# A transformer tower on one core: fewer constant products at the start, first loads on two queues, and one product for centring and gate

## The chip, the core and the metric

The kernel runs on one core of a Trainium2 chip. A core has TensorE (matrix products into PSUM), VectorE, ScalarE, GpSimd and SyncE (SP), each with its own instruction queue, and 16 DMA engines that they share. The engines meet through semaphores only: a queue stands still at an instruction whose wait isn't met. The metric is the time of one execution on the device in microseconds, taken as a median of several runs.

## What is computed

Four sequences of 1024 tokens with 64 features go through three layers: a gated retention layer, a state space layer and a mixture of experts, the last two with a residual and a layer norm ahead.

```python
q, k, v = x @ Wq + bq, x @ Wk + bk, x @ Wv + bv
retained = (d_gamma * (q @ k.T)) @ v
h = prelu(retained @ Wo + bo)

n = layernorm(h)
A_bar = exp(-softplus(n @ Wd + bd)); u = (1 - A_bar) * (n @ Wb + bb) * (n @ Wx + bx)
state = scan(state * A_bar + u)          # along the 1024 tokens
h = h + ((n @ Wc + bc) * state) @ Wy + by

n = layernorm(h)
logits = n @ gate_w + gate_b             # 16 experts, the best two, softmax over the two
h = h + sum(weight_e * (silu(n @ w1_e) * (n @ w2_e)) @ w3_e)
```

All is float32, but for the constant products and the counting.

## The kernel before

**Units.** The tokens are cut in four units (`UNITS`): two sequences (a half, `hh`) by 512 tokens of each. The two sequences lie one above the other on the 128 partitions (64 features each). A unit has 8 steps, one for each block of 128 key tokens. `scores(step)` makes q k products into two of the four `ring` banks, VectorE's `mix(step)` multiplies them by the decay `dg` into `mixed`, and `pv(step)` sums products with v in `acc`.

**What sets the order.** Each engine's program is written out in beats: a loop over `m`, and in each beat an engine issues the parts that are due. `BEAT` gives for each part its beats behind the end of its unit, a pair of numbers, the second one for the last unit. So the norms, the state space layer and the routing of a unit run between the scores of the next one. Expert work (`expert_piece`) begins in beat 65 and is mixed in behind the last unit's parts, piece by piece.

**The start.** SP issues the loads one after another: `wqk`, half of x for the first two sequences (`load_x(0, 0)`), `wvo` (for the product Wv Wo, which lets the kernel skip a product with Wo), `vecs` (all bias vectors), then the decay and the other parts of x. GpSimd writes the constants. TensorE's `warm_up(n)` issues n products of a constant bfloat16 matrix with itself, 128 columns, whose result nobody reads: `WARM` = 50, then the two wvo products (L1061, L1062), then `WARM2` = 20. Then come K and Q of the first 512 tokens (`project_kq`, L775), v of them (`project_v(0, 0)`, L785), the first scores (L802), and then v, K and Q of the second 512 tokens. VectorE copies the wvo product into `wv` and `row_v` (L1333 to L1335), and `take_v` adds the bias to v (L1130). ScalarE takes K and Q out of PSUM with their bias (`take_kq`, L587).

**The second norm.** `center2(u)` multiplies each 128 tokens of `hT` (tokens on columns) by the matrix `center_m`, identity less the mean, so the result stands with tokens on partitions, centred (L878, 4 products of 128 columns into bank 1 of `side`). Then 4 products of 32 columns with `gate_w`, the gate's weights with the centring already in them, give the raw logits in bank 0 (L882, `raw_done`). A float32 product is two passes in the profile, so each line shows x8. ScalarE's `take_raw` copies the centred rows to `n2` (L618), squares and sums them (L611; in the last unit L608 and VectorE's L1151), takes the root and scales the rows (L629). VectorE takes the reciprocal (L1159), scales the raw logits by it and adds the bias (`take_logits`, L1208, L1209), and picks the two best. `turn_h(u)` transposes `hT` into bank 1 (L889) once `take_raw` has read it; ScalarE's `take_h` takes that to `h`. The last unit's `center2` and `turn_h` are both at beat 17.

## Time and profile before

| | |
|---|---|
| median of 3 runs | 258.87 us (258.83 to 259.51) |
| profiled execution, its span | 331.5 us |
| TensorE busy in it | 257.1 us, 78% |
| VectorE, ScalarE, GpSimd busy | 48%, 36%, 30% |
| mean granted TensorE clock | 0.846 of full speed |
| chain that ended last, TensorE's share | 52% |
| chain that ended last, waits for what the profile doesn't name | 19% |

The profiled execution is one run and is 72.6 us longer than the median of the timed ones. Times of lines are read from the timeline (start, duration) in microseconds from the span's start, and the distance between the starts of two neighbours on TensorE is a better price for a product than its duration, since products overlap.

### The profile page before, as it was taken

The page shows a single profiled execution, that of the slowest core. Times are in us where ns is not written, and L with a number is a line of the kernel's source. Part 1 is how long each engine was busy: PE and PEld are TensorE (multiplying, and loading weights), DVE is VectorE, ACT ScalarE, POOL GpSimd, SP SyncE. Part 2 cuts the span into 40 slices and gives each one's busy share as a digit, 9 for nine tenths or more (in the row PEclk, how much of TensorE's full clock was granted, in tenths as well). Part 3 has the DMA queues.
Part 4 walks back from the last instruction along what each step waited for, and adds up shares of the span by engine and source line. Part 5 has one row for each costly group of instructions (what it writes and reads, how often), then busy time and mean ns, then how long its engine had stood idle before and what let it go on. Part 6 is the DMA issues. An engine that isn't in the chain of part 4 may idle for free.

```text
span 331.5 us, 4678 instructions
## 1 busy us (share of the span) xinstructions
PE 257.1 (78%) x1645; PEld 156.7 (47%) x1645; DVE 160.1 (48%) x283; ACT 119.7 (36%) x283; POOL 98.2 (30%) x119
## 2 busy tenths in 40 slices
PE   8999999988935976258829995169964899952995
PEld 7443332532411323136529884168642698621563
DVE  1453649789805993167705610053410466710664
ACT  1302561764108711467534541022320344311341
POOL 4000000004760077303771047600476000674000
PEclk9999999999985999658965997555796599995699
DMA  7999800000111101332221675995121323021101
GB/s 191 371 388 278 170 0 0 4 0 12 40 51 57 33 20 52 89 95 73 55 58 44 154 160 131 209 222 114 41 59 28 83 65 78 19 44 20 34 16 32
DMA packets 45990, 29.74 MB, mean 90 GB/s; under 512 B 32688, under 2 KB 41072, under 8 KB 45456
## 3 DMA queue, kind: packets, MB, share of 16 engines
q1 hardware_dynamic: 30416, 23.15, 27.1%
q10 hardware_dynamic: 12480, 3.15, 4.3%
q0 software_dynamic: 3072, 3.15, 3.9%
q8 instruction: 13, 0.21, 0.3%
q14 instruction: 9, 0.07, 0.1%
HBM read 20.46 MB, written 8.98 MB: 89 GB/s over the span
## 4 chain that ended last, share of the span: by engine, by line
PE 52%; another core or an unknown queue 19%; ACT 11%; DVE 10%; issue 7%; ACTq 0%; POOL 0%; DVEq 0%; POOLq 0%
PE ring L1013 10%; PE ring L971 9%; PE turn L988 7%; PE side L1025 5%; PE acc L816 4%; PE ring L802 4%; ACT squares L611 3%; PE side L843 3%; DVE mixed L1141 2%; PE ring L759 2%; PE side L775 2%; ACT n L629 2%; PE acc L934 1%; DVE state L1190 1%
## 5 line engine op out<-in xcount | busy, mean ns | idle before, releaser
L559 POOL DMA_INDIRECT slots<-n,slot_i x48 | 47.8, 996 | 121.9 <-DVE slot_i L1256 108.2
L1283 DVE TENSOR_TENSOR act<-ring,silu 128x512 f32<-128x512 f32 x56 | 38.4, 690 | 89.5 <-ACT silu L681 68.6
L569 POOL DMA_INDIRECT back_v<-results,slot_i x48 | 46.5, 968 | 81.4 <-DMA results<-res 67.7
L681 ACT ACTIVATE silu<-ring 128x512 f32<-128x512 f32 x56 | 33.3, 597 | 78.7 <-remote 38.5
L1141 DVE TENSOR_TENSOR mixed<-ring,dg 128x1024 f32<-128x1024 f32 x32 | 38.6, 1218 | 19.5 <-remote 10.9
L816 PE MATMUL acc<-mixed,v 128*64 128x512 f32 x128 | 34.3, 628 | 8.6 <-DVE mixed L1141 8.4
L802 PE MATMUL ring<-kq 64*128 64x512 f32 x128 | 33.5, 629 | 0.0
L1013 PE MATMUL ring<-nT,w_sb 64*128 64x256 f32 x128 | 24.2, 459 | 8.8 <-issue 8.0
L971 PE MATMUL ring<-slots_t,w_shared 64*128 64x128 f32 x192 | 19.8, 328 | 13.7 <-issue 12.7
L988 PE MATMUL turn<-w_sb,act 128*128 128x64 f32 (+1 forms) x192 | 29.1, 314 | 0.0
L988 PEld LDWEIGHTS turn<-w_sb,act 128*128 128x128 f32 x192 | 27.3, 226 | 3.0 <-issue 2.2
L971 PEld LDWEIGHTS ring<-slots_t,w_shared 64*128 64x128 f32 x192 | 16.7, 229 | 17.2 <-issue 17.1
L971 PE MATMUL ring<-slots_t,w_sb 64*128 64x128 f32 x192 | 18.3, 314 | 8.1 <-issue 7.9
L843 PE MATMUL side<-nT,wssm_sb 64*128 64x512 f32 x64 | 19.0, 673 | 3.8 <-DVE drive L1175 2.7
L1025 PE MATMUL side<-act,w_sb 128*64 128x256 f32 x128 | 19.6, 432 | 3.0 <-ACT sum_t L665 2.2
L1013 PE MATMUL ring<-dg,w_sb 64*128 64x256 f32 x128 | 21.9, 424 | 0.0
L971 PEld LDWEIGHTS ring<-slots_t,w_sb 64*128 64x128 f32 x192 | 15.4, 219 | 13.0 <-issue 12.7
L816 PEld LDWEIGHTS acc<-mixed,v 128*64 128x64 f32 x128 | 6.9, 137 | 28.3 <-DVE mixed L1141 17.1
L1013 PEld LDWEIGHTS ring<-nT,w_sb 64*128 64x128 f32 x128 | 12.4, 214 | 15.9 <-issue 10.8
L802 PEld LDWEIGHTS ring<-kq 64*128 64x128 f32 x128 | 11.3, 190 | 15.9 <-issue 13.5
L934 PE MATMUL acc<-ident,slots 128*128 128x128 f32 x48 | 9.4, 329 | 11.1 <-DMA slots<-slots 5.6
L595 ACT ACTIVATE hT<-acc,vec 128x512 f32<-128x512 f32 x4 | 2.7, 687 | 35.3 <-PE acc L816 25.3
(150 smaller groups left out, 306.5 us busy)
## 6 DMA issues: line engine op xcount, KB each, us to landing
dg<-dgT SPq DMA_DIRECT2D x8, 512.0 KB, 7.8
dg<-given SPq DMA_DIRECT2D x8, 512.0 KB, 15.7
slots<-zeros SPq DMA_DIRECT2D x3, 1024.0 KB, 13.2
w_shared<-w SPq DMA_DIRECT2D x48, 64.0 KB, 2.2
slots<-slots SPq DMA_DIRECT2D x12, 256.0 KB
results<-res ACTq DMA_DIRECT2D x12, 256.0 KB, 2.9
w_sb<-w SPq DMA_DIRECT2D x2, 1024.0 KB, 14.3
xs<-xT SPq DMA_DIRECT2D x4, 256.0 KB, 6.5
```

The lines of the kernel that those rows point to most:

```text
L559: pool.indirect_dma_start(out=slots_dram[r], out_offset=bass.IndirectOffsetOnAxis(ap=slot_i[:, r, k, i:i + 1], axis=0), in_=n2[:, u % 2, i ...
L569: pool.indirect_dma_start(out=back_v[:, r, i, k, :], out_offset=None, in_=results_dram[r], in_offset=bass.IndirectOffsetOnAxis(ap=slot_i[: ...
L681: s.activation(silu[:, n % 2], hidden_banks(n)[:, :, 0:PAIRS * P], ACT.Silu).then_inc(silu_done, 1)
L802: mm = pe.matmul(ring[:, 2 * (step % 2) + b, :], kq[rows_b(b), hh, 0, j * P:(j + 1) * P], kq[rows_b(b), hh, 1, th * CW:(th + 1) * CW], sta ...
L816: mm = pe.matmul(acc[rows_b(b), :], v[:, u // 2, j, b, :], mixed[:, step % MIX_BUFS, b, :], start=j == 0, stop=j == JT - 1)
L843: mm = pe.matmul(side[:, b, :], wssm_sb[rows_b(b), col:col + CH], nT[rows_b(b), :], start=True, stop=True)
L971: mm = pe.matmul(hidden_banks(p)[:, b, c:c + P], w[:, part * HID:(part + 1) * HID], slots_t[rows_b(b), n // 2 % 2, n % 2 * PAIRS + q, :], ...
L988: mm = pe.matmul(result_bank[:, (n % 2 * GB + k) * D:(n % 2 * GB + k + 1) * D], act[:, p % ACT_BUFS, k % 2, k // 2 * P:(k // 2 + 1) * P], ...
L1013: mm = pe.matmul(hidden_banks(p)[:, b, part * PAIRS * P:(part + 1) * PAIRS * P], w12_sb[rows_b(b), e, part * HID:(part + 1) * HID], x, sta ...
L1025: mm = pe.matmul(sum_bank[rows_b(b), :], w3_sb[:, e * D:(e + 1) * D], act[:, p % ACT_BUFS, b, :], start=e == 0, stop=e == NE - 1)
L1141: dve.tensor_tensor(mixed[:, step % MIX_BUFS], ring[:, r:r + 2, :], dg[:, u % 2, j, :].unsqueeze(1).broadcast_to([P, BH, CW]), ALU.mult).t ...
L1283: dve.tensor_tensor(act[:, n % ACT_BUFS], hidden_banks(n)[:, :, PAIRS * P:2 * PAIRS * P], silu[:, n % 2], ALU.mult).then_inc(act_done, 1)
```

## The change

1. `WARM` goes from 50 to 30 and `WARM2` is gone: 30 constant products instead of 70.
2. The loads of `vecs` and `wvo` are issued by ScalarE, ahead of its table load, and no longer by SP.
3. TensorE's start is in another order: K0 ahead of the wvo products, and v, K and Q of the second 512 tokens behind the scores of step 1 (beat 2) instead of step 0. VectorE's `take_v(0, 1)` comes behind its first `mix`.
4. The centring matrix and the gate's weights lie side by side in one tile `cg` of 160 columns. `center2` makes 4 products of 160 columns, two in each bank of `side`, where it made 4 of 128 and 4 of 32. `take_raw` reads both banks; `take_logits` scales the raw logits in two operations, a bank each, and waits for the centring's own semaphore.
5. `turn_h` writes a bank in which raw logits now stand, so it waits for `logits_done` as well. In the last unit it is two beats later (19).

```diff
-    "center2": (16, 17), "turn_h": (21, 17), "count": (24, 21), "owner_row": (27, 14), "prelu": (0, 0),
+    "center2": (16, 17), "turn_h": (21, 19), "count": (24, 21), "owner_row": (27, 14), "prelu": (0, 0),
...
+FIRST_PROJ_BEAT = 2
...
-WARM = 50
-WARM2 = 20
+WARM = 30
...
-            sp.dma_start(wvo_sb, wvo).then_inc(ld_wvo, 16)
-            sp.dma_start(vec[:, :], vecs).then_inc(ld_vec, 16)
             load_dg(0, 0)
...
-                s.activation(n2[:, u % 2].rearrange("p i d -> p (i d)"), side[:, 1, :], ACT.Copy).then_inc(raw_taken, 1)
+                s.activation(n2[:, u % 2].rearrange("p (k t b) d -> p k t (b d)", k=2, b=BH), cg_tiles()[:, :, :, 0:P],
+                             ACT.Copy).then_inc(raw_taken, 1)
...
+            s.dma_start(vec[:, :], vecs).then_inc(ld_vec, 16)
+            s.dma_start(wvo_sb, wvo).then_inc(ld_wvo, 16)
             s.wait_ge(consts_pool, 1)
...
-                    mm = pe.matmul(side[:, 1, t * P:(t + 1) * P], hT[:, u % 2, t * P:(t + 1) * P], center_m[:, :],
+                    mm = pe.matmul(side[:, t // 2, t % 2 * CG:(t % 2 + 1) * CG], hT[:, u % 2, t * P:(t + 1) * P], cg[:, :],
                                    start=True, stop=True)
                 mm.then_inc(cen_done[1], 1)
-                for t in range(TT):
-                    mm = pe.matmul(side[:, 0, t * 2 * NE:(t + 1) * 2 * NE], hT[:, u % 2, t * P:(t + 1) * P], gate_w[:, :],
-                                   start=True, stop=True)
-                mm.then_inc(raw_done, 1)
...
                 pe.wait_ge(raw_taken, u + 1)
+                pe.wait_ge(logits_done, u + 1)
...
             warm_up(WARM)
+            project_kq(0, "K0")
             pe.wait_ge(ld_wvo, 16)
...
-            warm_up(WARM2)
-            project_kq(0, "K0")
             project_kq(0, "Q0")
             project_v(0, 0)
             scores(0)
-            project_v(0, 1)
-            project_kq(0, "K1")
-            project_kq(0, "Q1")
-            pe.wait_ge(consts, 1)
 
             for m in range(BEATS):
                 for step in scores_at(m):
                     scores(step)
+                if m == FIRST_PROJ_BEAT:
+                    project_v(0, 1)
+                    project_kq(0, "K1")
+                    project_kq(0, "Q1")
+                    pe.wait_ge(consts, 1)
...
-                dve.wait_ge(raw_done, u + 1)
+                dve.wait_ge(cen_done[1], u + 1)
                 dve.wait_ge(scale_done, u + 1)
-                raw = side[:, 0, 0:UT * NE].rearrange("p (i e) -> p i e", e=NE)
-                link(dve.tensor_tensor(logits[:, :, :], raw, stats[:, 1, 2, :].unsqueeze(2).broadcast_to([P, UT, NE]), ALU.mult))
+                for k in range(2):
+                    i = slice(k * UT // 2, (k + 1) * UT // 2)
+                    raw = cg_tiles()[:, k, :, P:CG].rearrange("p t (b e) -> p t b e", b=BH)
+                    scale = stats[:, 1, 2, i].rearrange("p (t b) -> p t b", b=BH).unsqueeze(3).broadcast_to([P, UT // 4, BH, NE])
+                    link(dve.tensor_tensor(logits[:, i, :].rearrange("p (t b) e -> p t b e", b=BH), raw, scale, ALU.mult))
...
             take_v(0, 0)
-            take_v(0, 1)
             dve.wait_ge(consts, 1)
...
+                if m == FIRST_PROJ_BEAT:
+                    take_v(0, 1)
```

**TensorE at the start.** In the rows `ring<-ones` is a constant product, `acc<-mixed` a wvo product, `side<-xs,wqk_sb` a K or Q, `turn<-wv,xs` and `acc<-wv,xs` the v of the first and second 512 tokens, `ring<-kq` the scores. Before:

```order
L759 MATMUL ring<-ones 128x128 x49
L1061 MATMUL acc<-mixed 128x64 [waits ld_wvo]
L1062 MATMUL acc<-mixed 128x64
L759 MATMUL ring<-ones 128x128 x20
L775 MATMUL side<-xs,wqk_sb 128x512 [waits ld_x00,ld_wqk]
L775 MATMUL side<-xs,wqk_sb 128x512 [waits ld_x00]
L785 MATMUL turn<-wv,xs 128x128 [waits ld_x00,wv_done]
L785 MATMUL turn<-wv,xs 128x128 x3
L802 MATMUL ring<-kq 128x512 [waits kq_done]
L802 MATMUL ring<-kq 128x512
L785 MATMUL acc<-wv,xs 128x128 [waits ld_x01,wv_done]
L785 MATMUL acc<-wv,xs 128x128 x3
```

After:

```order
L766 MATMUL ring<-ones 128x128 x29
L782 MATMUL side<-xs,wqk_sb 128x512 [waits ld_x00,ld_wqk]
L1066 MATMUL acc<-mixed 128x64 [waits ld_wvo]
L1067 MATMUL acc<-mixed 128x64
L782 MATMUL side<-xs,wqk_sb 128x512 [waits ld_x00]
L792 MATMUL turn<-wv,xs 128x128 [waits ld_x00,wv_done]
L792 MATMUL turn<-wv,xs 128x128 x3
L809 MATMUL ring<-kq 128x512 [waits kq_done]
L809 MATMUL ring<-kq 128x512 x3
L792 MATMUL acc<-wv,xs 128x128 [waits ld_x01,wv_done]
L792 MATMUL acc<-wv,xs 128x128 x3
L782 MATMUL side<-xs,wqk_sb 128x512 [waits ld_x01,kq_done] x2
```

20 constant products are gone ahead of K0 and 20 behind the wvo products, which now stand behind K0; the scores of step 1 have passed v, K and Q of the second 512 tokens.

**VectorE at the same place,** from its last copy of the wvo product on; `v<-turn` and `v<-acc` are `take_v`; `mixed<-ring,dg` is `mix`. Before:

```order
L1335 COPY row_v<-acc 128x64
L1130 TENSOR_TENSOR v<-turn,row_v 128x512 [waits v_proj,wv_done]
L1130 TENSOR_TENSOR v<-acc,row_v 128x512 [waits v_proj]
L1141 TENSOR_TENSOR mixed<-ring,dg 128x1024 [waits scores_done,ld_dg0,consts]
L1141 TENSOR_TENSOR mixed<-ring,dg 128x1024 [waits scores_done]
```

After:

```order
L1342 COPY row_v<-acc 128x64
L1134 TENSOR_TENSOR v<-turn,row_v 128x512 [waits v_proj,wv_done]
L1145 TENSOR_TENSOR mixed<-ring,dg 128x1024 [waits scores_done,ld_dg0,consts]
L1134 TENSOR_TENSOR v<-acc,row_v 128x512 [waits v_proj]
L1145 TENSOR_TENSOR mixed<-ring,dg 128x1024 [waits scores_done]
```

The first `mix` has passed the second `take_v`.

**TensorE in the last unit,** round `center2`: `side<-ident,hT` is `turn_h`, `ring<-slots_t,w_shared` a hidden layer of four experts, `turn<-w_sb,act` a result, `acc<-ident,slots` a turn of the rows for the next experts. Before:

```order
L878 MATMUL side<-center_m,hT 128x128 x4
L882 MATMUL side<-gate_w,hT 128x32 x4
L889 MATMUL side<-ident,hT 128x128 x4
L957 TENSOR_LOAD owner_i
L971 MATMUL ring<-slots_t,w_shared 128x128 x8
L988 MATMUL turn<-w_sb,act 128x64 x8
L934 MATMUL acc<-ident,slots 128x128 x4
L957 TENSOR_LOAD owner_i
L971 MATMUL ring<-slots_t,w_shared 128x128 x8
```

After:

```order
L885 MATMUL side<-cg,hT 128x160 x4
L961 TENSOR_LOAD owner_i
L975 MATMUL ring<-slots_t,w_shared 128x128 x8
L992 MATMUL turn<-w_sb,act 128x64 x8
L938 MATMUL acc<-ident,slots 128x128 x4
L893 MATMUL side<-ident,hT 128x128 x4
L961 TENSOR_LOAD owner_i
L975 MATMUL ring<-slots_t,w_shared 128x128 x8
```

The gate's four products are gone, and `turn_h` has passed a hidden layer, a result and a turn of rows; its wait for the logits is new.

## Rows read from the trace of the kernel before

**Rows 1.** Page: head, granted TensorE clock by slice, shares of the last chain.

```profile
span 331.5 us, 4678 instructions
...
PEclk9999999999985999658965997555796599995699
...
PE 52%; another core or an unknown queue 19%; ACT 11%; DVE 10%; issue 7%; ACTq 0%; POOL 0%; DVEq 0%; POOLq 0%
```

**Rows 2.** Timeline, TensorE, start: start us, us, engine, line, operation, count.

```profile
1.23 4.60 PE L759 MATMUL ring<-ones 128*128 128x128 bf16 x50 [1.23 <-POOL ones L531]
...
6.35 1.29 PE L759 MATMUL ring<-ones 128*128 128x128 bf16 x20
...
7.47 1.94 PE L775 MATMUL side<-xs,wqk_sb 128*128 128x512 f32 x4
...
10.23 1.13 PE L802 MATMUL ring<-kq 64*128 64x512 f32 x4
```

**Rows 3.** Timeline, VectorE and ScalarE, same columns, first 14 us.

```profile
6.76 0.23 DVE L1334 COPY wv<-acc 64x64 f32<-64x64 f32 x1
...
7.02 0.23 DVE L1335 COPY row_v<-acc 128x64 f32<-128x64 f32 x1
...
8.68 1.46 ACT L587 ACTIVATE kq<-side,vec 128x512 f32<-128x512 f32 x2 [6.36 <-PE side L775]
```

**Rows 4.** DMA issues of SP; size and landing of wvo; landing of the load at 1.27.

```profile
1.27 0.42 SPq L414 DMA_DIRECT2D xs<-xT  x1
...
1.74 0.56 SPq L425 DMA_DIRECT2D mixed<-wvo  x1
...
mixed<-wvo SPq DMA_DIRECT2D x1, 80.0 KB, 2.6
...
DMA to landing us min/median/max: 2.6/2.6/2.6
```

**Rows 5.** Busy us by engine in a stretch, then granted clock, DMA share, GB/s.

```profile
2.00:3.00 1.00, 1.00 (x12) 1.00 (x10) 0.00 (x0) 0.30 (x2) 0.64 (x4) 1.00 0.88 284
...
13.00:36.00 23.00, 23.00 (x93) 7.98 (x91) 12.29 (x13) 4.12 (x6) 0.00 (x0) 1.00 1.10 322
```

**Rows 6.** Timeline round the second centring of unit 0.

```profile
59.80 1.16 PE L878 MATMUL side<-center_m,hT 128*128 128x128 f32 x8
...
60.50 0.68 ACT L596 ACTIVATE nT<-acc,der 128x512 f32<-128x512 f32 x1
...
60.79 0.98 PE L882 MATMUL side<-gate_w,hT 128*128 128x32 f32 x8
...
61.07 0.60 ACT L618 ACTIVATE n<-side 128x512 f32<-128x512 f32 x1
...
61.70 1.99 PE L802 MATMUL ring<-kq 64*128 64x512 f32 x8
...
62.87 1.23 DVE L1141 TENSOR_TENSOR mixed<-ring,dg 128x1024 f32<-128x1024 f32 x1 [0.91 <-PE ring L802]
```

**Rows 7.** Timeline, VectorE, the logits of unit 0 and what follows.

```profile
64.47 0.29 DVE L1208 TENSOR_TENSOR logits<-side,stats 128x128 f32<-128x128 f32 x1
...
64.80 0.29 DVE L1209 TENSOR_TENSOR logits<-logits,row 128x128 f32<-128x128 f32 x1
...
68.40 0.20 DVE L1166 RECIPROCAL stats<-stats 128x8 f32<-128x8 f32 x1 [1.08 <-ACT stats L622]
```

**Rows 8.** Timeline, the last unit: second centring, turn, logits.

```profile
165.79 0.98 PE L882 MATMUL side<-gate_w,hT 128*128 128x32 f32 x8
...
171.93 0.60 ACT L618 ACTIVATE n<-side 128x512 f32<-128x512 f32 x1 [2.29 <-remote]
...
172.58 1.11 PE L889 MATMUL side<-ident,hT 128*128 128x128 f32 x4 [5.82 <-ACT n L618]
...
177.96 0.29 DVE L1209 TENSOR_TENSOR logits<-logits,row 128x128 f32<-128x128 f32 x1
...
180.14 3.02 PE L971 MATMUL ring<-slots_t,w_shared 64*128 64x128 f32 x32
```

More of the change, by code:

```diff
@@ L67 @@
 VW, VB, VO, VCOLS = 0, 128, 256, 320
+CG = P + 2 * NE
 BEAT = {
@@ L235, in build_layer @@
         wgate_sb = sb("wgate_sb", [P, 2 * NE])
-        gate_w = sb("gate_w", [P, 2 * NE])
+        cg = sb("cg", [P, CG])
+        center_m, gate_w = cg[:, 0:P], cg[:, P:CG]
         wv = sb("wv", [P, P])
@@ L252, in build_layer @@
         ident = sb("ident", [P, P])
-        center_m = sb("center_m", [P, P])
         before = sb("before", [P, P], BF16)
@@ L328, in build_layer @@
         wy_done, hT2_done = sem("wy_done"), sem("hT2_done")
-        raw_done, logits_done = sem("raw_done"), sem("logits_done")
+        logits_done = sem("logits_done")
         h2_done, h_done = sem("h2_done"), sem("h_done")
@@ L378, in turned_sum, with cg_tiles @@
             return side[:, 1, 0:GB * D]
+        def cg_tiles():
+            return side[:, :, 0:2 * CG].rearrange("p k (t c) -> p k t c", c=CG)
         def count_bank(u):
```

## The prediction

> **What bounds the kernel now.** I read the head of the page first. The profiled execution spans 331.5 us, the timed median is 258.87 us. The chain that ended last holds 19% in "another core or an unknown queue", 0.19 x 331.5 = 63 us, and the clock row has a dozen slices of 5 to 7 tenths behind such stretches [rows 1]. 63 us of stalls and some 10 us of half-clock work account for the 72.6 us between the two numbers, so I take the timed runs to be nearly free of both. What lies around the span isn't shown. I price every edit in this execution's own microseconds, from stretches without a stall, and carry the difference over to the median.
>
> Then the start, in the timeline. TensorE begins at 1.23 us with 50 constant products, and the first scores start at 10.23 us [rows 2]. Everything in between is a queue in program order on one engine. From 13 to 36 us TensorE is busy in 23.00 of 23.00 us at full clock [rows 5]: whatever leaves its queue ahead of the first scores moves the rest forward one for one, until a load or an eviction is late.
>
> Then the stretch around the second centring of a unit, where the third edit lies [rows 6, 7]: there TensorE is mostly ahead, and ScalarE's long row of evictions and squares sets the pace. Last, the same place in the last unit [rows 8].
>
> **The change, part by part.**
>
> *Fewer constant products.* The 20 of the second lot start at 6.35 and the next product at 7.47: 1.12 / 20 = 56 ns each [rows 2]. The first 50 take 4.60 us with a tail of some 0.2, so 4.4; at 56 ns they would take 2.8. A slow one takes 128 columns at 1.2 GHz = 107 ns, 51 more, and 1.6 / 0.051 gives about 32 slow ones, so the clock rose from 1.2 to 2.4 GHz near 1.23 + 32 x 0.107 = 4.7 us, having been busy since 1.23. After the change 30 products end at 1.23 + 30 x 0.107 = 4.44 us, and the work that follows meets the rise instead. Where the rise falls before the first scores in both kernels, it doesn't matter which products are slow: 40 products' worth of columns is gone, and each is worth 56 ns at the end: 40 x 56 = **-2.24 us**. Bounds: nothing if a wait takes their place, and 40 x 0.107 = 4.3 if the clock rose only behind the first scores in both. I take 2.24, since the row shows the rise at 4.7.
>
> *Waits that could take their place.* (a) K0 now wants its load at 4.44. It was issued at 1.27 and landed 2.6 later, at 3.87 [rows 4]: 0.57 us to spare, where it had 3.6. (b) The wvo products now come behind K0, near 5.5 (K0 is half of the 1.94 us of four passes, less than 0.97, plus 0.15 for its slow part). wvo landed at 1.74 + 2.6 = 4.34; from ScalarE's queue, which is free at about 0.8, it is issued second, behind vec, at 1.4: about 4.0. (c) V(0,0) wants the second copy of wv on VectorE, which ended at 6.99 [rows 3] with the wvo products issued from 5.76 on; shifted with them it ends near 6.8, and Q0 keeps TensorE busy to 7.0. (d) The first scores want Q0's eviction, which ended at 10.14, and they began at 10.23 [rows 2, 3]; Q0 and V(0,0) keep their distance, so both move together. (e) ScalarE issues two DMAs ahead of its table load, about 1 us; its first eviction is due after 5.5. Nothing. (f) SP loses two issues, so each later load is issued 1.2 us earlier, half of what its user moves; between 13 and 36 us no product waited for one. None of these costs in my sum.
>
> For (a) the stretch from 2 to 3 us moved 284 GB/s [rows 5], and wvo is 80 KB [rows 4]: 0.28 us if all of it went ahead of the x load. The Trainium skill (DMA: Bandwidth & Descriptors, "Issuing engines are not separate DMA queues") says that two queues share the same 16 engines and interleave, so a second queue saves issue time and no bandwidth. By that rule x lands at up to 4.15 and not at 3.87, still ahead of 4.44: the sum stays, the spare time halves.
>
> *Projections behind the first scores.* The two scores pairs are issued together, V(0,1), K1 and Q1 behind them; VectorE takes v of the second half after its first `mixed`. The same work in another order on an engine that never idles there [rows 5]: 0. If a wait hid in that stretch the order could earn up to 0.3 us; if VectorE's first `mixed` came too late for the third scores it would cost, but its scores now end at about 9.1 and the third scores come near 12.9.
>
> *One product instead of two.* Centring takes 60.79 - 59.80 = 0.99 us, the gate 61.70 - 60.79 = 0.91 [rows 6]. A pass of 128 columns goes by every 112 ns (0.91 / 8), and a pass of 32 columns as well; by columns, one of 512 takes 1.94 / 4 = 0.485 at most [rows 2], so 160 columns cost 160/512 of that, 0.15, or 0.134 without its tail. I take 22 ns more for each of 8 passes, +0.18. TensorE saves 0.91 - 0.18 = 0.73 us in each of four units, 2.9 us in all. Who gets it? In unit 0 the scores behind it start at 61.70 and their `mixed` at 62.87 after 0.91 us idle on VectorE [rows 6]; moved forward, VectorE idles later instead, because the next thing it has is the reciprocal for ScalarE's squares. So 0 of it reaches the end in units 0 to 2; the other end is all of it, -0.73 each.
> What ScalarE waits for is the centring alone, and that ends 0.18 later: 59.80 + 1.16 = 60.96 before, 61.14 after. ScalarE is free at 60.50 + 0.68 = 61.18, its copy started at 61.07 [rows 6]. That is +0.1 a unit on the engine that sets the pace, **+0.3** for three; between 0 and 0.5.
> VectorE takes the logits in two operations of 64 columns: 0.23 each and 0.26 from start to start for such a one [rows 3], where one of 128 took 0.29, and 0.33 to the next [rows 7]: 2 x 0.26 - 0.33 = +0.19. Behind it VectorE stood idle for 1.08 us before 68.40, for ScalarE [rows 7]. That cover hides it in units 0 to 2; without it, +0.6 in all.
>
> *The last unit.* Before, the turn of h stands straight behind the gate (166.77) and waits for ScalarE's copy of 171.93; TensorE idles 5.82 us, nearly all of it a stall of ScalarE ("remote") [rows 8]. Without the stall the copy would end about when the gate does, so little is freed there. Now the turn comes two beats later, behind one hidden, one result and one turn of slots, and it waits for the logits too. They end at 178.25, which is 178.25 - 172.53 = 5.7 us behind the copy; TensorE got from the turn to the next hidden, at 180.14, in 180.14 - 172.58 = 7.6 us, much of it at half clock [rows 8]. At full clock it would be there in 4 to 5 us, so the turn may have to wait up to 1 us, and behind it in TensorE's queue stand two hidden products for which ScalarE and VectorE wait. Those hidden products need a product of VectorE that comes after the same logits, so most of the wait exists already. I take **+0.2**, between -0.8 (all that TensorE saves is kept) and +0.8 (the 0.6 us turn and the 0.19 us on VectorE both land on the path).
>
> Sum: -2.24 + 0.3 + 0.2 = -1.7. This execution would span 331.5 - 1.7 = 329.8 us without its chance stalls; the median goes from 258.87 to **257.1 us**.
>
> **The rivals.**
> *TensorE's saving counts.* If in the timed runs TensorE is behind in the units' later parts, two or three of the four 0.73 us come through: -2.24 - 1.5 to -2.24 - 2.2, 254.4 to 255.1 (edge of the case: 256.2). For it: TensorE was on 52% of the last chain [rows 1]. Against: around the product itself the chain's pace is ScalarE's, and the 0.91 us idle of VectorE is followed by another wait [rows 6, 7].
> *The start gains half or less.* Evictions, the copy of wv or the loads take the place of the products removed (a to d), 0.6 to 1.7 us of them, and the units cost their +0.5: 258.1 to 259.5. For it: four things are due within 0.6 us of each other where 3.6 us were spare. Against: each of them is early by the rows.
> *Slower: a gap ahead of K0.* If the x load lands behind 4.44 us, TensorE stands idle while its clock is still low. The gap costs its own length, and the rise comes later: it came after 3.5 us of unbroken work from 1.23 on. Counted anew from the gap, it moves from 4.7 to at least 8, and work in 3.3 us at 1.2 GHz is half done: +1.7. Slower than before from a gap of 0.1 to 0.6 us on (gap + 1.7 + 0.5 against 2.24); with a gap of 1.0, 258.87 - 2.24 + 0.5 + 1.7 + 1.0 = 259.8. For it: the spare time is 0.3 to 0.57 us. Against: the load landed at 3.87 with a queue of the same loads behind it. The Trainium skill (TensorE: Matmul & The Clock Gate, "The HAM clock gate") says that the clock rises only after sustained work and that the moment differs from run to run; no row here shows a start with a gap, so the size of this is open, and the price above is from the one rise that the trace shows.
> That the change doesn't do what it says is excluded at the main places: the rows of the order show 30 products, the loads on ScalarE's queue, and products of 160 columns.
>
> **How the numbers follow.** Forecast 257.1 (256.2 to 258.0): 0.56. TensorE's saving counts: 0.18. Half or less: 0.16. Gap: 0.10. 0.3% of 258.87 is 0.78 us, about what a measurement of this kernel can tell from no change: faster is below 258.1, slower above 259.65. The first two cases are faster, with a sliver of the third: 0.75. The third is mostly within, with the gap's smaller values: 0.17. Slower: 0.08. The range 254.8 to 258.9 holds the forecast, four fifths of the second case and half of the third, 0.56 + 0.15 + 0.10 = 0.81.
>
> **What would show it.** After the change, in the timeline: 30 products from 1.23 to about 4.4, K0 straight behind them with no idle time, the first scores at 8.0 instead of 10.23. If they start there, the start's term holds; at 9 or later one of (a) to (d) failed, and the row ahead of it names which. In a unit's stretch: centring with 8 passes in 1.17 us, ScalarE's copy 0.1 later behind its neighbour, VectorE's idle time before the second reciprocal 0.9 and not 1.08. In the last unit: the turn behind the slots, and what it waits for. The prediction is wrong if the distance from the first scores to the end of unit 0 changes by more than 0.3 us, or if the stalls of the profile turn out to be in the timed runs too and move with the code.

## The result, and the profile after

The changed kernel takes **269.18 us** (median of 4 runs, 268.27 to 271.27), the kernel before 259.19 beside it (4 runs, 258.83 to 262.89): **1.041 times as long**, 95% interval 1.036 to 1.047. Forecast were 257.1 us and faster. The profiled execution took 269.49 us and spans 267.4.

One thing must be said ahead of all else. Over a whole session on a chip every kernel here takes either about 260 us or about 327 us; the profile that the prediction read (331.5 us of span, [rows 1]) is of the long kind, the timed runs shown with it and the result are of the short kind. Times below are compared within one session, traces also across the short sessions. The runs of the kernel before in a short session lie in two groups, in the fifth session 255.85 to 258.45 us (mean granted clock 0.964 to 0.977) and 261.07 to 262.88 us (0.948 to 0.954), and a ratio compares only the shorter runs of each kernel, so it differs from that of the medians.

First the page of the changed kernel: its span, the granted clock by slice, the shares of the last chain by engine.

```profile
span 267.4 us, 4543 instructions
...
PEclk9999999999999979995799899986966999999999
...
PE 56%; DVE 15%; DMA 10%; ACT 10%; issue 7%; SPq 1%; ACTq 0%; POOL 0%; DVEq 0%; POOLq 0%
```

"Another core or an unknown queue", 19% of the chain in [rows 1], is gone; a DMA has 10%, and that is new. The timeline of TensorE at the start (start us, us, engine, line, operation, count), against [rows 2]:

```profile
1.23 3.37 PE L766 MATMUL ring<-ones 128*128 128x128 bf16 x30 [1.23 <-POOL ones L535]
4.40 1.11 PE L782 MATMUL side<-xs,wqk_sb 128*128 128x512 f32 x2
...
7.97 1.99 PE L809 MATMUL ring<-kq 64*128 64x512 f32 x8
```

The first scores stand at 7.97 instead of 10.23, 2.26 us earlier, and the distance from them to ScalarE's first `hT` is the same, 26.17 us in both. Unit 0's second centring, in the timelines of TensorE, ScalarE and VectorE, against [rows 6, 7]:

```profile
57.53 1.35 PE L885 MATMUL side<-cg,hT 128*128 128x160 f32 x8
...
58.92 0.60 ACT L622 ACTIVATE n<-side 128x512 f32<-128x512 f32 x1
...
66.25 0.20 DVE L1170 RECIPROCAL stats<-stats 128x8 f32<-128x8 f32 x1 [0.88 <-ACT stats L627]
```

The copy starts 1.39 us behind the product instead of 1.27, and VectorE idles 0.88 instead of 1.08. The centring starts 1.29 us ahead of the scores behind it (57.53 to 58.82), where centring and gate together took 1.90 (59.80 to 61.70). So far nearly everything is as forecast. Then comes a stretch that the prediction never read. ScalarE's timeline from 172 us on: `res` is a copy of a pair of expert results out of PSUM, `results<-res` its store to DRAM.

```profile
172.79 0.60 ACT L692 ACTIVATE res<-turn 128x512 f32<-128x512 f32 x1 [1.32 <-PE turn L992]
173.42 0.37 ACTq L695 DMA_DIRECT2D results<-res  x1
176.71 0.60 ACT L692 ACTIVATE res<-turn 128x512 f32<-128x512 f32 x1 [1.32 <-PE turn L992]
177.33 0.37 ACTq L695 DMA_DIRECT2D results<-res  x1
197.66 0.60 ACT L692 ACTIVATE res<-turn 128x512 f32<-128x512 f32 x1 [11.42 <-DMA results<-res]
```

There are two `res` buffers, so the eighth copy needs the landing of the sixth store. It waits 11.42 us for it. What SP issues around that store (the given sums go to DRAM and are then spread over the partitions, 8 DMAs of 512 KB):

```profile
170.39 0.80 SPq L457 DMA_DIRECT2D given<-mixed  x2
172.62 5.67 SPq L465 DMA_DIRECT2D dg<-given  x8
```

The spread is issued 0.80 us ahead of the sixth store.

### The profile page after: what moved, and what is told of

Its sections match the earlier page's. It is cut to its first block, busy times and chain, and to the rows that moved or that the text cites. A ratio compares the mean times of both kernels' runs of the same rounds, so it can differ in the third digit from the quotient of the medians.

```text
span 267.4 us, 4543 instructions
## 1 busy us (share of the span) xinstructions
PE 229.9 (86%) x1573; PEld 136.1 (51%) x1573; DVE 160.9 (60%) x287; ACT 119.6 (45%) x283; POOL 98.7 (37%) x119
## 4 chain that ended last, share of the span: by engine, by line
PE 56%; DVE 15%; DMA 10%; ACT 10%; issue 7%; SPq 1%; ACTq 0%; POOL 0%; DVEq 0%; POOLq 0%
PE ring L1017 11%; DMA results<-res 9%; PE ring L975 8%; PE side L1029 6%; PE turn L992 6%; PE acc L823 5%; PE ring L809 5%; PE side L850 4%; ACT squares L615 3%; DVE state L1194 3%; DVE mixed L1145 2%; PE side L782 2%; PE acc L938 2%; DVE drive L1179 1%; ACT n L634 1%
## 5 line engine op out<-in xcount | busy, mean ns | idle before, releaser
L1017 PE MATMUL ring<-nT,w_sb 64*128 64x256 f32 x128 | 22.9, 435 | 15.0 <-DVE act L1290 15.0
L823 PE MATMUL acc<-mixed,v 128*64 128x512 f32 x128 | 34.1, 627 | 0.2
L992 PE MATMUL turn<-w_sb,act 128*128 128x64 f32 (+1 forms) x192 | 24.0, 278 | 0.0
L992 PEld LDWEIGHTS turn<-w_sb,act 128*128 128x128 f32 x192 | 22.3, 191 | 2.7 <-issue 1.6
L1017 PE MATMUL ring<-dg,w_sb 64*128 64x256 f32 x128 | 21.0, 406 | 0.0
L1029 PE MATMUL side<-act,w_sb 128*64 128x256 f32 x128 | 18.2, 408 | 0.0
L692 ACT ACTIVATE res<-turn 128x512 f32<-128x512 f32 x12 | 7.2, 597 | 24.0 <-PE turn L992 12.6
L1303 DVE TENSOR_TENSOR dg<-dg,nT 128x512 f32<-128x512 f32 x16 | 10.3, 687 | 7.9 <-DMA dg<-given 7.9
L1017 PEld LDWEIGHTS ring<-dg,w_sb 64*128 64x128 f32 x128 | 13.8, 205 | 1.7
L975 PE MATMUL ring<-slots_t,w_shared 64*128 64x128 f32 x192 | 13.9, 295 | 0.2 <-issue 0.2
L975 PEld LDWEIGHTS ring<-slots_t,w_sb 64*128 64x128 f32 x192 | 12.4, 197 | 3.0 <-issue 2.3
```

Of the source, the lines that this page charges most:

```text
L823: mm = pe.matmul(acc[rows_b(b), :], v[:, u // 2, j, b, :], mixed[:, step % MIX_BUFS, b, :], start=j == 0, stop=j == JT - 1)
L975: mm = pe.matmul(hidden_banks(p)[:, b, c:c + P], w[:, part * HID:(part + 1) * HID], slots_t[rows_b(b), n // 2 % 2, n % 2 * PAIRS + q, :], ...
L992: mm = pe.matmul(result_bank[:, (n % 2 * GB + k) * D:(n % 2 * GB + k + 1) * D], act[:, p % ACT_BUFS, k % 2, k // 2 * P:(k // 2 + 1) * P], ...
L1017: mm = pe.matmul(hidden_banks(p)[:, b, part * PAIRS * P:(part + 1) * PAIRS * P], w12_sb[rows_b(b), e, part * HID:(part + 1) * HID], x, sta ...
L1029: mm = pe.matmul(sum_bank[rows_b(b), :], w3_sb[:, e * D:(e + 1) * D], act[:, p % ACT_BUFS, b, :], start=e == 0, stop=e == NE - 1)
```

## The experiments

**Sessions.** Median of the kernel before in each: first session 327.12 us (25 runs), second 330.47 (19), third 261.96 (19), fourth 326.44 (29), fifth 261.07 (11). The second and the fifth were on the same chip.

*The first session: the change in two parts.* `e1` is the kernel before itself, `e2` has of the diff only the start (30 constant products, two queues, the projections behind the scores), `e3` only the merged product with the turn at beat 19; their cores, and that of `e4`:

```diff
# e2, against the kernel before
-WARM = 50
-WARM2 = 20
+WARM = 30
+                if m == FIRST_PROJ_BEAT:
+                    project_v(0, 1)
# e3, against the kernel before
+                    mm = pe.matmul(side[:, t // 2, t % 2 * CG:(t % 2 + 1) * CG], hT[:, u % 2, t * P:(t + 1) * P], cg[:, :],
# e4, against the changed kernel
-            s.dma_start(vec[:, :], vecs).then_inc(ld_vec, 16)
-            s.dma_start(wvo_sb, wvo).then_inc(ld_wvo, 16)
+            sp.dma_start(wvo_sb, wvo).then_inc(ld_wvo, 16)
+            sp.dma_start(vec[:, :], vecs).then_inc(ld_vec, 16)
```

> The kernel before, unchanged, for an undisturbed trace. In the changed kernel's trace one store of results issued by ScalarE at 173.4 us lands 24 us later, beside eight loads of the spread weights (dg<-given) that SP issued from 172.6 us, and TensorE, VectorE and ScalarE stand still for some 20 us between 174 and 200 us. Theory A (the store is caught behind that burst in the changed kernel only): here the same store is issued ahead of the burst or lands in under 15 us, and the stretch from the burst's issue to the next expert results is about 12 us shorter. Rival B (the loss lies before the burst, in the units): the burst is issued 8 us or more earlier than in the changed kernel. Time 258 to 260 for both.

> Only the start is changed: 30 constant products, loads of vecs and wvo from ScalarE, projections behind the first scores; the second norm is as before. If the start alone tips the burst (theory A by timing or by the use of ScalarE's queue): 266 to 270. If the product of 160 columns or the later turn does it: 256.5 to 257.5, which is before less 2.2.

> Only the second norm is changed: one product of 160 columns, logits in two operations, the last unit's turn of h two beats later; the start is as before, 70 constant products and all loads from SP. If the second norm's part tips the burst: 269 to 272. If the start does it: 258.5 to 260.5.

> The changed kernel with the loads of vecs and wvo back in SP's queue, nothing else. If using ScalarE's queue at the start is what slows the later stores on that queue: 257 to 259. If not: 268 to 270, as the changed kernel.

Measured: 326.8, 325.55, 328.37 and 324.5 us; ratios 0.997 (0.993 to 1.002), 0.995 (0.991 to 0.999), 0.996 (0.990 to 1.002), 0.988 (0.981 to 0.996). No forecast was met, since all were made for the short time. With the long time nothing was slower, so none of this speaks of the loss on record. The second session ran the two kernels whole:

> The kernel before once more. The first four kernels ran on a chip where it took 327 us in every run, and the measurement of the change on one where it took 259. If that is a property of the chip or of the session, this one lands at 258 to 263 or at 324 to 332 in all its runs, and at 259 its trace has no stall of ScalarE and VectorE of 5 us or more without a named releaser ahead of 150 us. Theory A: there the store of results that overlaps the spread of weights lands in under 15 us.

> The changed kernel, unchanged. Where before takes 259: 268 to 271 and the store of results beside the burst takes 20 us or more, as in the profile after. Where before takes 327: 323 to 326, because both kernels then wait in the same long stalls and the change shows only its 2.2 us at the start.

> Only the start is changed. Where before takes 259: 256.5 to 257.5 if the second norm's part makes the loss, 266 to 270 if the start does. Where before takes 327: 324 to 326.

331.21 (1.001), 327.13 (0.987, 0.982 to 0.991) and 328.66 us. The forecasts for the long time, 323 to 326 us for `e6` and 324 to 326 for `e7`, came out 1 to 3 us too low. The same code that lost 4.1% gains 1.3% here. The waits of ScalarE in `e5`, the kernel before with 332.4 us of span (us in total, times, longest):

```profile
ACT silu L681 <- remote: 32.8, 6, 17.2
...
ACT n L618 <- remote: 19.5, 3, 10.9
...
ACT slots_t L675 <- remote: 9.4, 1, 9.4
```

The traces of all kernels of the long sessions have such waits, and none of the short ones has one. They cover just the stretch in which the short runs lose. In the trace of [rows 1] the longest of them stands between the spread and the sixth store (timelines of SP and of ScalarE):

```profile
202.87 5.37 SPq L461 DMA_DIRECT2D dg<-given  x8
...
217.64 0.60 ACT L681 ACTIVATE silu<-ring 128x512 f32<-128x512 f32 x1 [16.86 <-remote]
...
218.75 0.37 ACTq L690 DMA_DIRECT2D results<-res  x1
```

The spread is issued 15.88 us ahead of the store there, so this trace could not show what happens where the two are close; only a short session could.

*The third session: short, the same four-way split.*

> The kernel before, on whatever chip comes. If the run is one of the short ones (about 259 us), its trace shows what the stretch from take_given to the second store of results looks like without the change: by theory A (the loss of the changed kernel is the spread of the given sums, 4 MB, getting ahead of a store of results, 24.15 us to its landing in the changed kernel) every store of results here lands within 10 us of its issue and the last token tile's expert work begins 8 to 10 us earlier; by rival B (the loss lies in the units) the spread is issued here some 8 to 10 us earlier than 172.6 us. If it is one of the long ones (about 327 us), it says only that the length goes with the chip or the hour and not with the kernel.

> The changed kernel on the same chip. Where the kernel before takes 259 us, both theories expect 267 to 271 us, and a store of results with over 20 us to its landing by theory A alone. Where the kernel before takes about 327 us, a ratio of 0.985 to 0.997, as on the two chips before.

> Only the edits of the start (30 constant products, two queues, the other projections behind the first scores). Where the kernel before takes 259 us: if the start moves the spread against the stores, 267 to 271 us here and no loss in the merged product alone; if the merged product or the turn at beat 19 does it, 257 us. Where it takes 327 us: 0.993 to 0.999 of it.

> Only the merged product of centring and gate logits, with the turn of h at beat 19. Where the kernel before takes 259 us: 267 to 271 us if the merged product or the turn makes the loss, 258.5 to 259.5 us if the start makes it. Where it takes 327 us: 0.993 to 1.000 of it.

| kernel | median us (lowest to highest, runs) | ratio, interval |
|---|---|---|
| before (all its runs) | 261.96 (256.12 to 264.05, 19) | |
| `e8` before | 260.21 (256.31 to 263.84, 10) | 0.999, 0.992 to 1.007 |
| `e9` changed | 263.38 (261.99 to 267.01, 5) | 1.019, 1.010 to 1.028 |
| `e10` start only | 258.83 (252.78 to 265.45, 11) | 0.989, 0.981 to 0.998 |
| `e11` merged product only | 263.19 (260.55 to 264.57, 4) | 1.023, 1.013 to 1.032 |

No median met the forecast for the short time; the changed kernel's was 267 to 271 us. The spread of `e8` is issued at 174.16, not 8 to 10 us before 172.6, and that rules rival B out; its eighth copy stands at 192.07, 5.6 us ahead of the profile after. The start alone gains 1.1%, about its forecast (2.24 of 258.87 us, 0.9%). For `e9` and `e11` the ratios are clear of 1 but not of 2%, and `e11` has four runs; its traced run spans 258.5 us and that of `e8` 259.4, so as a whole those two traces show no loss. But no run of a kernel with the merged product is shorter than 259.71 us in the short sessions, while the others go down to 252.78. What the merged product costs can be read in the last unit. TensorE in `e11`, then `e8`:

```profile
145.35 1.35 PE L886 MATMUL side<-cg,hT 128*128 128x160 f32 x8
...
151.53 1.09 PE L894 MATMUL side<-ident,hT 128*128 128x128 f32 x4 [1.35 <-DVE logits L1217]
152.54 3.08 PE L976 MATMUL ring<-slots_t,w_shared 64*128 64x128 f32 x32
```

```profile
146.73 1.16 PE L878 MATMUL side<-center_m,hT 128*128 128x128 f32 x8
147.72 0.98 PE L882 MATMUL side<-gate_w,hT 128*128 128x32 f32 x8
148.58 0.66 PE L889 MATMUL side<-ident,hT 128*128 128x128 f32 x4
...
153.12 2.06 PE L971 MATMUL ring<-slots_t,w_shared 64*128 64x128 f32 x32 [0.43 <-DVE act L1283]
```

Before, the turn of h runs straight behind the gate, because the logits lie in another bank. Merged, the logits of half the tiles lie in the bank that the turn writes, so it waits 1.35 us for VectorE to read them, two beats later. The 32 hidden products behind it take 3.08 us instead of 2.06: the clock has gone to half. The same in windows: busy us of each engine with instructions, then granted clock, DMA share, GB/s, for the 5 us ahead and the 3.4 us behind. The changed kernel (the profile after), then `e8`:

```profile
146.20:151.20 5.00, 3.82 (x39) 3.28 (x37) 2.21 (x7) 4.44 (x6) 4.06 (x4) 1.00 0.08 28
151.20:154.60 3.40, 3.23 (x24) 2.93 (x26) 2.87 (x9) 1.42 (x4) 2.49 (x4) 0.50 0.97 235
```

```profile
146.40:151.40 5.00, 5.00 (x54) 4.59 (x51) 1.59 (x4) 3.91 (x6) 3.83 (x4) 1.00 0.16 48
151.40:154.80 3.40, 2.97 (x42) 2.77 (x43) 3.23 (x10) 2.89 (x5) 2.62 (x3) 1.00 0.36 89
```

TensorE was busy for 3.82 of the 5 us ahead with the change and for 5.00 without, and only in the first does the clock fall to 1.2 GHz, for 3.4 us. From the second to the third store of results it takes 6.10 us in `e11` and 4.46 in `e8`: **+1.6 us**, in every kernel with the merged product (6.08 to 6.19) and in none without (4.45 to 4.46).

A second half-clock piece stands 10 us behind the end of unit 2's attention. The changed kernel, then `e11`:

```profile
91.60:96.60 5.00, 3.17 (x18) 1.37 (x16) 3.94 (x8) 3.74 (x25) 3.53 (x4) 1.00 0.38 114
96.60:100.00 3.40, 3.40 (x8) 0.39 (x6) 3.13 (x12) 2.00 (x4) 0.00 (x0) 0.50 0.25 72
```

```profile
93.80:98.80 5.00, 3.17 (x18) 1.37 (x16) 3.95 (x8) 3.74 (x25) 3.51 (x4) 1.00 0.39 115
98.80:102.30 3.50, 3.50 (x16) 0.76 (x14) 3.23 (x12) 2.09 (x5) 0.00 (x0) 1.00 0.25 73
```

Both were busy for 3.17 us ahead; without the merged product it is 3.90 or 3.91 (`e10`, `e8`). ScalarE's third `hT` to its fourth takes 29.99 to 30.04 us in the four short traces that have the start and the merged product, 28.32 to 28.43 in the four others: **+1.6 us**. What TensorE no longer does is idle time there (1.83 us ahead of the turn of n instead of 1.09), and the clock fell behind it in four of the five traces with the merged product. Why not in `e11` stays open, and that the idle time is the reason is not shown.

*The late store.* Eight short traces, ordered by how far the spread is issued behind the sixth store (the one at 173.42 above; in all of them it is the sixth):

| trace | sixth store issued | spread issued | behind it by | wait of the eighth copy for a store |
|---|---|---|---|---|
| profile after | 173.42 | 172.62 | -0.80 | 11.42 |
| `e9` changed | 173.24 | 172.56 | -0.68 | 7.52 |
| `e10` start only | 169.79 | 169.13 | -0.66 | 10.03 |
| `e17` changed | 174.00 | 173.43 | -0.57 | 7.61 |
| `e16` changed, ordered | 174.32 | 174.38 | +0.06 | none |
| `e18` start only, ordered | 167.70 | 167.76 | +0.06 | none |
| `e11` merged only | 173.55 | 173.91 | +0.36 | none |
| `e8` before | 173.09 | 174.16 | +1.07 | none |

`e16` to `e18` are told below. The start alone brings the store forward by 3.30 us (`e10` against `e8`) and the spread by 5.03: from the second store of the given sums to the spread it takes 3.7 us in `e8` and 3.0 in `e11`, and 1.8 to 2.1 in the profile after, `e9`, `e10` and `e17`. So the store that went 1.07 us ahead of the spread in the kernel before goes 0.6 to 0.8 us behind it. Of the kernels that set this order freely, each trace with the new start (four) has the spread first, and neither of the two without it has. Why the landing of the given sums is shorter with the new start no run tells.

*The fourth session: fix the order of spread and store, move the turn.* `e12` and `e13` let SP wait ahead of the spread for the sixth copy of results:

```diff
                 sp.wait_ge(mixed_done, ALL_STEPS)
+                sp.wait_ge(res_read, 6)
```

`e14` moves the turn of the last unit by a beat:

```diff
-    "center2": (16, 17), "turn_h": (21, 19),
+    "center2": (16, 17), "turn_h": (21, 20),
```

> The changed kernel, and SyncE waits before the spread of the given sums (8 x 512 KB) for the copy ahead of the sixth store of results, so that this store is issued first. Theory A (where the spread is issued even 0.7 us ahead of that store, the store lands over 20 us later and ScalarE's next copy waits 7.5 to 11.4 us for it): no such wait here, the copy ahead of the eighth store at about 192 us instead of 196 to 198.3, and 4 to 8 us less than the changed kernel on the same chip, 255 to 260 us where the kernel before takes 259 to 262. Rival E (the loss is the half clock alone, and the late store only rides on it): within 1.5 us of the changed kernel.

> Only the edits of the start, with the same wait before the spread. The trace of the start alone had the late store (10.0 us of wait at the copy, 263.7 us of span), while its shortest run took 252.8 us. Theory A: no wait at the copy, and 253 to 257 us where the kernel before takes 259 to 262. Rival E: as the start alone, 0.98 to 0.997 of the kernel before.

> The changed kernel with the last unit's turn of h at beat 20 instead of 19, behind the next piece of expert work. Theory F (the merged product costs in the last unit: the turn waits 1.36 us for the logits, and the clock is half for the 3.4 us behind it): no wait at the turn, no half clock at 151 to 155 us, 1.3 to 2.5 us less there. The late store (theory A) can fall either way, since both are moved: the store issued 1.5 us earlier would be ahead of the spread unless the spread moves as much. By rival E 1.5 to 3 us less in all.

> The changed kernel beside its variants, for the comparison on one chip: 1.01 to 1.045 of the kernel before where that takes 259 to 262 us, with the late store; 0.985 to 0.997 where that takes about 327 us.

It was a long session: 327.07 (0.989, 0.984 to 0.993), 331.62 (1.013, 1.008 to 1.019), 326.69 (1.001, 0.997 to 1.005) and 324.02 us (0.993, 0.990 to 0.996). There the turn at beat 20 is slower than at 19, the wait ahead of the spread gains nothing with the whole change and makes the start alone slower than the kernel before (1.013). The traces show what the wait does there: it holds the spread back for a store that stands behind a stall, to 208.21 us in `e12` where `e15` issues it at 195.84. Of the short sessions this says nothing.

*The fifth session: short, the fixed order again.*

> As the run of this kernel before: the changed kernel, with SyncE waiting before the spread for the copy ahead of the sixth store of results. Where the kernel before takes about 260 us, theory A: ScalarE's copy ahead of the eighth store waits for no store, this copy at about 192 us instead of 196 to 198.3, and 4 to 8 us less than the changed kernel beside it (255 to 260 us). Rival E: within 1.5 us of the changed kernel. Where the kernel before takes about 327 us, it tells nothing of either: 0.985 to 1.0.

> The changed kernel on the same chip: 1.01 to 1.045 of the kernel before where that takes about 260 us, with a wait of 7 to 12 us at the copy ahead of the eighth store; 0.985 to 0.997 where that takes about 327 us.

> Only the edits of the start, with the wait before the spread. Where the kernel before takes about 260 us, theory A: no wait at the copy, and 253 to 257 us, the shortest of all kernels here; rival E: as the start alone, 0.98 to 0.997 of the kernel before. Where that takes about 327 us: 1.00 to 1.02, as on the chip before.

Measured: the changed kernel `e17` 268.41 us (260.55 to 270.98, 6 runs), with the order kept `e16` **260.82** (259.71 to 261.48, 6), the start alone with the order kept `e18` **255.85** (253.02 to 260.59, 6). The kernel before has 261.07 (255.85 to 262.88, 11); the ratios are 1.014 (1.009 to 1.018) for `e16` and 0.989 (0.982 to 0.997) for `e18`. One wait on SP takes 7.6 us off the changed kernel, as theory A forecast ("4 to 8 us less"), and rules out rival E ("within 1.5 us"). `e18` meets both forecasts, and without the fixed order the start alone had the same ratio, 0.989 (`e10`), so what the wait gives the start alone is not shown. `e16` and `e18` differ by the merged product alone: 5.0 us by medians, 2.7 in the spans of the traces (259.2 and 256.5). Its last chain, `e17` (start us, us, what):

```profile
173.37 0.61 ACT res L692
173.98 0.02 issue
174.00 22.58 DMA results<-res
...
196.66 0.61 ACT res L692
```

and the eighth copy of `e16`, in ScalarE's timeline:

```profile
191.83 0.60 ACT L693 ACTIVATE res<-turn 128x512 f32<-128x512 f32 x1 [1.41 <-PE turn L993]
```

4.83 us earlier, and behind TensorE, not behind a store. The spans of the two traces are 6.4 us apart (265.6 and 259.2), the rest of it behind this copy. How the store comes to take 22.58 us is seen in its packets. A store of results is 1024 packets of 256 bytes on ScalarE's queue; this counts those that start in each 3 us (stores 6 and 7 together):

```
us from       173   176   179  182  185  188  191  194   197
e16, ordered  565   450     9   14   81   89   89  105  1634
e17             0   764   109   79   72   94   84  172  1698
```

In `e16` the 1024 packets of the sixth store have started 5.6 us after its issue (in `e8` they all start from 174.0 to 175.3). In `e17` the first of them starts at 177.2, 3.2 us after the issue (0.9 in `e16`), when the spread runs at its full rate already; 764 get through by 179, and then 24 to 36 a us beside the 8 KB packets of the spread, until that is done at 197. In `e16` the seventh store meets this fate instead, but its buffer is wanted only by the ninth copy, after 209. The Trainium skill says (DMA: Bandwidth & Descriptors, "Queues, rings and completion order") that each DMA engine goes round the queues for which it has work, one packet at a time. The trace is near to that: from 179 to 191 us of `e17` 354 packets of 256 bytes start beside 281 of 8 KB, so the stores' queue gets more than half of the packets and 4% of the bytes. Whether the profile counts the same packets as the page is not shown.

The rest of the loss is the clock again. TensorE in 190.5 to 200.5 us of the profile after, and in 190.7 to 200.7 of `e16`:

```profile
190.50:200.50 10.00, 0.28 (x2) 0.31 (x4) 1.12 (x2) 1.68 (x3) 0.00 (x0) 0.75 0.83 184
```

```profile
190.70:200.70 10.00, 10.00 (x84) 7.17 (x85) 6.31 (x10) 4.64 (x8) 0.00 (x0) 1.00 1.05 233
```

In the first TensorE stands still for nearly all of it and works at half clock from 195.6 to 205.8 us. Until 255 us the clock is at half for 20.5 us in `e8`, `e11` and `e18`, for 27.3 in `e16`, and for 34.1 in the four traces with the late store.

## Why the prediction was wrong

**The base.** It took the timed runs to be nearly free of the 63 us of stalls and of the half clock. For the stalls this holds in the short session of the result: its profile has no such wait. For the half clock it doesn't: 20.5 us in `e8`, the kernel before, and 34.1 in the profile after. And it carried a sum made in one condition into the other, though the stalls had stood over the very stretch in which the short runs lose. The last item of its own list, that "the stalls of the profile turn out to be in the timed runs too", is what the long sessions show.

**The start, -2.24 us.** Right: 2.26 in the profile after. There K0 stands straight behind the constant products (4.40), none of the waits (a) to (e) came, and alone the start measured 0.989 (`e10`). The rival's gap ahead of K0 did come in the fifth session, 0.23 us in `e18` and 0.24 in `e17` (TensorE):

```profile
4.84 1.21 PE L782 MATMUL side<-xs,wqk_sb 128*128 128x512 f32 x2 [0.24 <-DMA xs<-xT]
```

K0 starts 0.44 us later than in the profile after and the first scores 0.54 (8.51 against 7.97), no later than the 8.53 of `e16`, which has no gap; K0 took 1.21 us in `e17` and 1.67 in `e16`. The rival's 1.7 us for a later rise of the clock did not come. The rise, which the prediction put near 4.7 us, lies between 3.9 and 6.9 in the traces (50 products took 4.53 us in `e11` and 5.41 in `e8`), which moves all behind it by up to 1 us from run to run. The clock's records begin at this rise, at 4.7 us in the trace of [rows 1], and not at about 16 us as the section on the time before has it.

**Item (f), SP loses two issues, and "moves the rest forward one for one".** This is the step that failed most. (f) asked only whether a load comes too late and put nothing in the sum; the rule at the start let all that follows keep its distances. Neither asked what SP issues later on and what that runs ahead of. The sixth store moved forward by 3.30 us and the spread by 5.03 (`e10` against `e8`), so the bulk transfer that SP issues 170 us later passed a store of another queue: 7.6 us by `e16` against `e17`. Which of the start's edits moved it, the two issues taken from SP or the rest, is not shown.

**Units 0 to 2, +0.3 us.** The mechanism was right, the 0.12 us is there in unit 0, and TensorE's saving reached nobody, as forecast. The saving is 1.90 - 1.29 = 0.61 us a unit and not 0.73: a pass of 128 columns had taken 0.99 / 8 = 124 ns (the prediction divided the gate's 0.91 instead), one of 160 takes 1.29 / 8 = 161, 37 ns more and not 22. What the sum left out is the clock: +1.6 us once, behind unit 2, in kernels with the whole change, where TensorE idles more ahead of it.

**The last unit, +0.2 us, at most +0.8.** It named the wait for the logits ("up to 1 us") and measured 1.36. It took most of it to exist already; in fact the turn had stood free of the logits and straight behind the gate. With the half clock behind it the term is +1.6 us, twice the upper bound.

The sum with these sizes is -2.3 + 0.1 + 1.6 + 1.6 = +1.0 us without the late store, and with its 7.6 us +8.6; measured were +10.0 beside the profile after, +1.4 in the third session and +7.3 in the fifth, by medians. `e16`, without the late store, stands 0.25 us under the kernel before by medians and 1.4% over it by the ratio; +1.0 us (0.4%) lies between, and the only short trace of the kernel before is of a run of 261.16 us. The terms of the merged product, 0.1 + 1.6 + 1.6 = 3.3 us, are less than the 5.0 between `e16` and `e18`; where the rest lies is open. What part of the changed kernel's runs has the late store is not known: only traces show it, and three of three did, but in the third session the traced run (267.01 us) is the longest of five and the others took 261.99 to 263.58, and in the fifth one of six took 260.55 us, like `e16`.

**The rivals.** Slower had 0.08, and that by another mechanism. The right one, a change of order between two queues that share the DMA engines, would have needed the question of (f) asked of every later bulk transfer. (A slip in its working: half of the third case's 0.16 is 0.08 and not 0.10, so the chances in the range add up to 0.78.)

Not settled: what makes a session long or short; whether the second queue alone moves the spread (`e4` was run only with 327 us); whether beat 20 or a bank of its own for the logits would save the 1.6 us of the last unit in a short session; why the kernel before itself takes from 256 to 263 us in a short session.

## What to carry to other kernels

An edit at the start moves all that is issued later, each queue by its own amount: list the bulk transfers of each queue, and for each small store or load of another queue that someone waits for, how far ahead of the burst it is issued. Here the margin was 1.07 us, and the edit moved the two against each other by 1.73. A wait can fix the order, but it also holds the burst back where the store is late (12 us in `e12`). Where an engine saves work but not time, look at the granted clock behind the new idle time and at what shared bank the merged result now blocks. When a profile holds long stalls that the timed runs don't have, read the sum as good up to the first of them only. The best kernel in the short sessions is the start alone, without the merged product: 0.989 by the ratio with and without the fixed order, and with it 255.85 us against 261.07 by medians.

## What the hardware showed beyond that

The same kernel took 330.47 us and, in a later session on the same chip, 261.07: in the long condition ScalarE, VectorE and SP wait for up to 17 us at a time with no named releaser (17.2, 11.0 and 16.1 us at most in `e5`) and no run here says why. During the first long one, 90 to 101 us, GpSimd issues indirect DMAs until 98.7. In that condition the ratios of the short one don't hold, not even in sign. And a 256 KB store of results lands in 2.3 to 4.4 us away from the burst, in 6.7 (`e16`) and 7.3 (`e18`) when the 4 MB burst is issued 0.06 us behind it on another queue, and in 22.58 to 24.15 when the burst was issued 0.6 to 0.8 us ahead of it. The next store, 3.9 us behind the burst in `e18`, takes 22.6 as well.
